# Sparse attention on one core: three small operations of VectorE in another order

## The reference, cut to what matters

```python
dots = jnp.einsum('bhid,bhjd->bhij', q, k) * SCALE        # j: 16 memory slots, then the tokens
dots = jnp.einsum('bhij,hk->bkij', dots, pre_proj)
dots = jnp.where(causal, NEG_INF, dots)
thresh = jax.lax.top_k(dots, 64)[0][..., -1:]
dots = jnp.where(dots < thresh, NEG_INF, dots)
attn = jax.nn.softmax(dots, axis=-1)
out = jnp.einsum('bhij,bhjd->bhid', attn, v)
```

## Time and profile before

| | us |
|---|---|
| median of 3 runs | 2828.13 |
| the runs | 2826.66 to 2834.22 |
| the profiled execution | 2827.18 |
| its span | 2824.8 |
| VectorE busy | 2330.4 (82% of the span) |
| TensorE busy (matmuls) | 2226.8 (79%) |
| ScalarE busy | 1433.0 (51%) |
| GpSimd busy | 309.2 (11%) |
| mean granted clock of TensorE | 0.886 |

### The profile page before, as it was taken

The page is one execution under the profiler, slowest core; times in us unless marked ns, Lnnn a source line. Parts: engine busy times, 40 slices in busy tenths (PEclk is TensorE's granted clock), DMA queues, the critical chain, the costliest instruction groups (busy, mean ns, idle before and its releaser), DMA issues.

```text
span 2824.8 us, 34520 instructions
## 1 busy us (share of the span) xinstructions
PE 2226.8 (79%) x10182; PEld 1305.2 (46%) x10182; DVE 2330.4 (82%) x9115; ACT 1433.0 (51%) x2207; POOL 309.2 (11%) x299
## 2 busy tenths in 40 slices
PE   6599456767777757888888888899994999973997
PEld 2555334434444424444444445455552454542664
DVE  2504599999999989999999999999999999965445
ACT  1121234444555535666666667666763767751221
POOL 0000001111111111111111111111100010110000
PEclk7699667778888878999999999999997999986998
DMA  2000000000000000000000000000000000001000
GB/s 64 1 1 1 0 1 1 1 1 1 1 1 1 1 0 1 1 1 1 1 1 1 1 1 1 1 1 1 1 1 0 1 1 1 1 1 53 1 1 15
DMA packets 15427, 11.52 MB, mean 4 GB/s; under 512 B 6893, under 2 KB 13687, under 8 KB 15223
## 3 DMA queue, kind: packets, MB, share of 16 engines
q1 hardware_dynamic: 11184, 6.82, 0.9%
q10 hardware_dynamic: 4038, 2.37, 0.3%
HBM read 8.14 MB, written 1.05 MB: 3 GB/s over the span
## 4 chain that ended last, share of the span: by engine, by line
DVE 63%; PE 25%; ACT 5%; issue 4%; DVEq 2%; ACTq 0%; POOL 0%; POOLq 0%
DVE cand L1155 16%; DVE R L1204 10%; DVE r L1206 9%; DVE F L1217 5%; DVE W L1185 4%; PE bank L951 4%; DVE W L1184 4%; PE bank L871 4%; PE bank L839 3%; PE bank L959 2%; PE bank L855 2%; ACT R L581 2%; ACT R L570 2%; DVE W L1177 1%; PE bank L755 1%
## 5 line engine op out<-in xcount | busy, mean ns | idle before, releaser
L839 PE MATMUL bank<-hT,qT 128*128 128x512 f32 (+3 forms) x1280 | 577.6, 589 | 247.1 <-ACT R L543 204.3
L1155 DVE MAX8 cand<-R 128x8 f32<-128x12 f32 (+15 forms) x4096 | 667.8, 223 | 5.3 <-ACT R L543 5.1
L871 PE MATMUL bank<-WP,Y 128*128 128x512 f32 x1088 | 600.5, 636 | 74.4 <-ACT WP L588 72.2
L839 PEld LDWEIGHTS bank<-hT,qT 128*128 128x128 f32 x1280 | 241.2, 207 | 500.4 <-ACT R L543 236.4
L855 PE MATMUL bank<-ident,R 128*128 128x128 f32 x2176 | 442.9, 286 | 14.7 <-ACT R L581 14.7
L588 ACT ACTIVATE WP<-bank 128x512 f32<-128x512 f32 x544 | 320.4, 594 | 258.5 <-PE bank L856 250.6
L581 ACT ACTIVATE R<-R,negm 128x144 f32<-128x144 f32 (+15 forms) x256 | 309.4, 1211 | 235.2 <-DVEq L1301 235.2
L856 PE MATMUL bank<-nidentb,F 128*128 128x128 bf16 x2176 | 413.3, 225 | 0.0
L855 PEld LDWEIGHTS bank<-ident,R 128*128 128x128 f32 x2176 | 318.4, 146 | 145.0 <-issue 102.4
L421 POOL TENSOR_TENSOR Zs<-Zs,rden 128x508 f32<-128x508 f32 x64 | 135.9, 2124 | 2240.5 <-DVE rden L1213 2240.5
L543 ACT ACTIVATE R<-bank 128x1024 f32<-128x1024 f32 (+7 forms) x384 | 290.0, 772 | 164.9 <-PE bank L839 87.8
(11 more groups left out here) (233 smaller groups left out, 2299.8 us busy)
## 6 DMA issues: line engine op xcount, KB each, us to landing
R<-in_L_attn_Wkv ACTq DMA_DIRECT2D x2, 512.0 KB, 8.3
R<-in_L_ffn_gate_w SPq DMA_DIRECT2D x1, 1024.0 KB, 6.8
R<-in_L_ffn_up_w SPq DMA_DIRECT2D x1, 1024.0 KB, 9.4
out<-X SPq DMA_DIRECT2D x1, 1024.0 KB, 5.1
R<-in_L_attn_Wq ACTq DMA_DIRECT2D x1, 512.0 KB, 6.7
WP<-in_L_attn_Wo ACTq DMA_DIRECT2D x1, 512.0 KB, 10.9
R<-in_L_ffn_wi SPq DMA_DIRECT2D x1, 256.0 KB
R<-in_L_ffn_wo SPq DMA_DIRECT2D x1, 256.0 KB
```

What stands on the lines that cost most here:

```text
L839: last = pe.matmul(to, qT[:, k % 2, i, :], hT[:, a:b], start=True, stop=b < n, skip_group_check=True)
L871: pe.matmul(bank[6], Y[:, j, :], PT[:, (blocks_before(k) + j) % 4, :], start=(j == 0), stop=(j == k // 4))\
L1155: mark(dve.max(cand[:, :, c, i], lists(S[:, k % NS, i, 0:n], n, c)))
```

## The change

`memory_weights` of the group before moves into `pivots`, between `negm` and `cutb`; `negm` moves behind `cutt`; the separate signal on `s_cut` becomes an increment on the `cutb` instruction itself, followed by a wait for it; `weigh_heads` of the group two before moves into stage 13 of the merge, behind its three MAX8 and ahead of the wait.

```diff
--- before.py
+++ after.py
@@ -1161,6 +1161,8 @@
                     mark(ins)
                     stage = done[0]
                     list_step(k + 1, 3 * step, 3)
+                    if k >= 2 and step == 13:
+                        weigh_heads(k - 2)
                     dve.wait_ge(s_dve, stage)
                     return step + 1
 
@@ -1189,12 +1191,16 @@
                 dst = W16[:, 1 - flip, 0:CUT * GU].rearrange("p (r u) -> p r u", u=GU)
                 beside(step, dve.tensor_tensor(dst, src[:, 0:CUT, 0, :], src[:, CUT - 1::-1, 1, :], ALU.max))
                 link(dve.tensor_reduce(piv[:, :], dst.rearrange("p r u -> p u r"), AX.X, ALU.min))
+                mark(dve.tensor_scalar(cutt[:, :], piv[:, :], -BIG_ * LOW * (1 - NEAR), BIG_ * LOW * SLACK,
+                                       ALU.mult, ALU.add))
+                cut = done[0]
                 mark(dve.tensor_scalar(negm[:, k % 2, :], top[:, :], -1.0 / LOW, None, ALU.mult))
-                link(dve.tensor_scalar(cutt[:, :], piv[:, :], -BIG_ * LOW * (1 - NEAR), BIG_ * LOW * SLACK,
-                                       ALU.mult, ALU.add))
-                link(dve.scalar_tensor_tensor(out=cutb[:, k % 2, :], in0=piv[:, :], scalar=-BIG_ * LOW * (1 + NEAR),
-                                              in1=cutt[:, :], op0=ALU.mult, op1=ALU.max))
-                dve.sem_inc(s_cut, 1)
+                if k >= 1:
+                    memory_weights(k - 1)
+                dve.wait_ge(s_dve, cut)
+                dve.scalar_tensor_tensor(out=cutb[:, k % 2, :], in0=piv[:, :], scalar=-BIG_ * LOW * (1 + NEAR),
+                                         in1=cutt[:, :], op0=ALU.mult, op1=ALU.max).then_inc(s_cut, 1)
+                dve.wait_ge(s_cut, k + 1)
 
             def below(k, i):
                 u, n = GU * k + i, wide(k // 4)
@@ -1310,10 +1316,6 @@
             list_step(0, 0, CH * GU)
             for p in range(NG):
                 pivots(p)
-                if p >= 1:
-                    memory_weights(p - 1)
-                if p >= 2:
-                    weigh_heads(p - 2)
                 for i in range(GU):
                     below(p, i)
                 threshold(p)
```

## The result

The changed kernel takes 2859.68 us in the median of five runs (2851.24 to 2863.59), the kernel before 2827.11 us beside it (five runs, 2825.50 to 2834.22): ratio 1.0101, 95% interval 1.0084 to 1.0117, estimated over all the runs (the two medians alone would give 1.0115). That is 1% slower, outside the predicted range.

A forecast was written before the change was run, and what follows sets the result against it. VectorE, 95% busy from 430 to 2150 us, was taken as the bound; -16.6 - 9.3 + 26.1 + 1.6 + 0.6 + 0.3 = +2.7 us gave 2829.9 us profiled, 2830.8 us median, range 2812 to 2848.

The forecast's parts named there:

- +26.1 us: Groups 2 to 55: time VectorE loses to GpSimd's operations beside the last merge stages and small instructions; bounds +5 to +31.
- Part 2: GpSimd's four operations move with the reciprocal: 9.3 us of loss on long scans goes, +26.1 us comes at the merge's end.
- 21.3 us: Last merge instruction (L1190) blocked by GpSimd's first operation: mean 0.395 us a group over 54 groups.
- 4.8 us: Pm or cutb hit by GpSimd from group 24 on, 0.24 falling to 0.06 us, 32 groups.
- R: Start of the reciprocal, moved into merge stage 13; the forecast counts group 38's times from it.
- Part 1: VectorE from piv to first long scan: new order and signal save net 0.30 us a group, -16.6 us in all.
- The removed 9.3 us: Loss of the long scans to GpSimd in groups 2 to 55, said to vanish with the reciprocal's move.
- Part 3: Reciprocal's earlier wait for Zs: +1.6 us in group 55, +0.6 in 62; later cut in group 56, +0.3.
- (a): Rival, chance 0.22: GpSimd and VectorE's 16-bit instructions pass each other; 2809.7 us, or 2816.7 with small instructions in the way.
- (c): Rival, chance 0.05: the waits are free, so taking them away saves nothing; 2847.4 us.
- (b): Rival, chance 0.10: GpSimd wins against stage 14's second merge instruction; 28.6 us more, 2859.4 us.
- Theory A: Experiments' theory: GpSimd's four operations, released inside the merge, keep VectorE out, costing more than the rest saves.

The follow-up runs named there:

- after_again: The changed kernel run again with nothing altered: 2854.77 us, ratio 1.0103 to the kernel before.
- gpsimd_empty: The changed kernel with GpSimd's four operations a group replaced by one memset: 2797.33 us, ratio 0.9880 to the kernel before.
- The pair without GpSimd: The changed kernel with and without the reciprocal's move, GpSimd's four operations replaced by one memset in both: 2797.33 us with the move, 2799.86 us without.
- recip_stage_11: The changed kernel with the reciprocal in merge stage 11 in place of 13: 2859.07 us, ratio 1.0095 to the kernel before.
- signal_only: The kernel before with the signal to ScalarE put on the cutb instruction and nothing else: 2816.04 us, ratio 0.9958.
- order_only: The changed kernel with the reciprocal taken out of the merge, back behind cutb: 2809.08 us, ratio 0.9931 to the kernel before.
- recip_only: The kernel before with the reciprocal alone moved into merge stage 13: 2870.41 us, ratio 1.0144.
- gpsimd_late: The changed kernel with GpSimd's first operation held until VectorE's first MAX8 of a threshold row is through: 2814.21 us, ratio 0.9940 to the kernel before.

## Why the prediction was wrong

**The step that failed is "+26.1 us" of Part 2.** Groups 2 to 55 lost 48.5 us to collisions with GpSimd's operations. Of its two terms the merge instruction was nearly right: "21.3 us" for the last merge instruction, and 24.5 was measured. A blocked 16-bit instruction ends 0.14 us after GpSimd's operation in group 38; the formula taken from the long scans had it end 0.06 after. The term for the small instructions, "4.8 us", was wrong by five times: 24.0 us, the first scan's 0.9 among them.

- The price was charged for one meeting, of the third operation with Pm or cutb, from group 24 on; the fourth operation has no place in the sum at all. In the trace the small instructions are hit in every group, two of them in 41 of the 54; in group 38 the fourth operation (1424.13) is the one that stretches cutb. GpSimd's gaps are 0.08 us, and VectorE's whole tail from L1192 to the first scan runs beside the four operations.
- The stretch of one blocked instruction moves the next ones into the next operation. That feedback wasn't in the sum, which put each instruction at its undisturbed place behind L1192. In group 38 the prediction has cutt at R+2.27, ahead of the third operation at R+2.34; in the trace, where L1192 lost 0.41 for 0.33, both start at R+2.32, and cutt was hit in place of Pm.
- Four-element instructions with one input (cutt, negm, r9) are kept out as well; cutt takes 0.47 for 0.16. The text had this as the upper bound, "+31 if the four-element instructions too are kept out", and even the bound was 17.5 us too low, because of the two points above.

With 48.5 in place of 26.1 the predicted sum for the profiled run is 2829.9 + 22.4 = 2852.3; 2851.6 was measured, and 2848.7 in after_again. One term was wrong; the rest adds up to within a microsecond in the first trace and 4 us in the second.

**Part 1 was right.** The first scan was forecast 1.07 us after piv; without collisions it starts 1.08 after (gpsimd_empty), for 1.47 before; the means over groups 2 to 55 are 1.09 and 1.48. Less 0.08 for the reciprocal in the merge (1421.29 to 1421.37) that is 0.31 a group for "0.30", 16.7 us over the 54 groups. Its parts were off against each other: the separate signal 0.18 for 0.12, the rest less.

**The removed 9.3 us were right:** the stretch of the scans in groups 2 to 55 went from 9.7 to 0.9 us.

**Part 3 happened where it was forecast, and its size is not settled.** Group 55's reciprocal waited 1.75 us for "+1.6", but only 0.45 in after_again. Groups 58 to 62 waited 1.33, 1.81, 2.82, 1.11 and 1.55, while piv 55 to piv 63 took 410.0 us (408.9 in after_again) for 408.8 before. The pair without GpSimd has 1.3 us for all of Part 3, forecast 2.5; two traces of one kernel differ by 2.5 there, so that this agreement proves little. That "a VectorE that is 2 us later delays nobody" holds up to about that size: at 3 to 5 us of waiting, in recip_stage_11, the same groups took 15 us more.

**The rivals.** (a) is refuted: the 16-bit instruction is kept out as the 32-bit ones are. (c) is refuted by signal_only and order_only. (b) named 2859.4 us, close to the median, but its mechanism didn't happen: the second instruction of stage 14, L1187, stays at 0.28 us in group 38 and grows by 0.02 at the most in any group; GpSimd asks behind it, at 1421.59. The agreement is chance. Theory A of the experiments stands in this form: the loss is the reciprocal's place through GpSimd. Moving it alone costs what order and signal can't pay (recip_only), taking GpSimd's operations out or holding them back gives it all back (gpsimd_empty, gpsimd_late), and its size depends on which instructions lie under the operations (recip_stage_11).

**What stays open** is the 8.1 us by which the median of the changed kernel exceeds its profiled run. Executions of these kernels differ in the first stretch, before the sparse attention starts: first piv between 339.0 us and 350.3 us in the traces. No trace of a slower run of the changed kernel exists, so this isn't shown to be the cause. The clocks on record lean that way in the first set: its three slower runs have mean granted clocks of 0.889 to 0.893, its two faster ones 0.883 and 0.884, and a first stretch of 60 us at 1.00 in place of 0.73 would by itself (an estimate from the two rows at the end of this text) add 0.006 to the mean. In after_again they don't: its fastest run has 0.890.

## What to carry to other kernels

A signal that is moved ahead moves all the work that it releases, on another engine, and that work must be laid beside the instructions it will now run with, one by one and with their delays fed back: here 0.3 us a group were saved on VectorE and 0.9 us a group lost to GpSimd. Here a chain of short operations was a bad neighbour for a chain of short instructions; put such operations, by a semaphore, beside instructions that they don't disturb (here MAX8, 1.51 us for 1.03). A bound for "kept out" is worked out for the case in which every instruction in the stretch is hit, not only the one due at the first meeting.

## What the hardware showed that was not expected

- GpSimd keeps out VectorE instructions of four elements with a single input as well: cutt 0.47 us for 0.16 and negm 0.47 for 0.16 (recip_only), r9 in groups 15 to 34 of the changed kernel. MAX8 and the reduction beside the same operations were not stretched by more than 0.03 (piv 0.36, 0.37 before); the reciprocal never ran beside them. The Trainium skill (SBUF — State Buffer, "SBUF: two separate sides") tells of an exclusive lock on shared ports, taken by VectorE instructions with two SBUF inputs, against GpSimd operations that read SBUF, and by those in a two-port mode, which it says tensor_scalar can enter. The trace agrees for L1192 (0.67 us for 0.26); for cutt, negm and r9, all tensor_scalar, it is only consistent with it, as no run here changes their mode. So the rule that the prediction drew on for two inputs already had room for the one-input instructions that it left at their upper bound.
- A few hundredths of a microsecond decide who keeps the other out, and the recorded starts don't tell the winner. In order_only the first GpSimd operation, started 0.05 us after a short scan, made it take longer than its elements give (144 elements: 0.37):

```profile
402.27 1.25 DVE L1208 SCALAR_TENSOR_TENSOR R<-R,r 128x144 f32<-128x144 f32 x1
```

```profile
402.32 1.03 POOL L421 TENSOR_TENSOR Zs<-Zs,rden 128x508 f32<-128x508 f32 x1 [16.96 <-DVE rden L1217]
```

The scan was recorded first and lost, where the operations three and four of recip_stage_11 came 0.01 and 0.03 behind and lost themselves. In order_only GpSimd's first operation is recorded 0.05 or 0.06 us behind the first scan in 61 of the 62 groups from 2 to 63, and got in ahead of it in four (3, 15, 22, 51; the scan takes 0.87 or 0.88 longer); in the kernel before it is so in three (15, 56, 62). "Whichever starts first keeps the other out", as the prediction put it, is thus not what the recorded starts show at this distance.

- The granted TensorE clock of the first 60 us (the third column from the right, ahead of DMA share and GB/s) differs between executions. In gpsimd_empty it is 1.00, that is 2.4 GHz throughout, and the first piv is at 350.1 us:

```profile
0.00:60.00 60.00, 39.11 (x78) 18.75 (x78) 9.00 (x51) 8.08 (x13) 5.18 (x43) 1.00 0.31 75
```

In the changed kernel it is 0.73, and the first piv is at 342.9:

```profile
0.00:60.00 60.00, 38.86 (x81) 18.77 (x82) 8.99 (x51) 8.68 (x15) 5.16 (x43) 0.73 0.31 75
```

In all three traces with 1.00 (gpsimd_late and signal_only are the others) the first piv is at 349.8 us or later, in the rest it is at 348.05 or earlier. In these twelve traces a high clock at the start went with a later start of the sparse attention; why was not tried.
